# Conditioning clamps one unit earlier, a re-ordered opening with its products on GpSimd, activations laid out by batch, and the second batch's gates inside the unit loop

## The reference

```python
def bi_wkv(r, k, v, w, u, c):            # called twice: w = cond, then cond2; k = v = f
    tf = sigmoid(sum(c)); decay = exp(-exp(w)) * (0.5 + 0.5 * tf)
    ek = exp(min(k, 30)); ekv = ek * v
    nf, df = forward scans  of ekv, ek:  a = a * decay + x_t
    nb, db = backward scans of ekv, ek
    euk = exp(min(u + k, 30))
    return sigmoid(r) * (nf + nb - ekv + euk * v) / max(df + db - ek + euk, 1e-8) * (0.8 + 0.2 * tf)

y   = bi_wkv(x, f, f, ...)               # the cond stage
x  += W_O @ softmax(mask(K Q^T) / sqrt(128)) V        # 16 heads of 128, from y, causal
y2  = bi_wkv(x, f, f, ...)               # the cond2 stage
out = x + sum over the top 2 of 8 experts of gate * (y2 @ expert_w + expert_b)
```

## Time and profile before

| what | value |
|---|---|
| median of 3 runs | 398.97 us |
| the profiled execution | 399.12 us |
| its span | 397.3 us |
| TensorE busy | 366.3 us, 92% of the span |
| DVE / ACT / POOL busy | 306.8 / 224.5 / 187.5 us |
| mean granted TensorE clock | 0.991 of full speed |

### The profile page before, as it was taken

How to read it: one execution, slowest core, us unless ns; L and a number is a source line. 1 busy time by engine, 2 the same in 40 slices (tenths; PEclk the granted TensorE clock), 3 DMA queues, 4 the chain that set the end, 5 groups by cost and what they waited for, 6 DMA issues and landing times.

```text
span 397.3 us, 7668 instructions
## 1 busy us (share of the span) xinstructions
PE 366.3 (92%) x2600; PEld 340.9 (86%) x2600; DVE 306.8 (77%) x836; ACT 224.5 (57%) x613; POOL 187.5 (47%) x213
## 2 busy tenths in 40 slices
PE   0886989998999899979998999899999999999996
PEld 0775979998999899979997999899999989777885
DVE  4999978887787888778878887888757583677565
ACT  4647777557756757575767665866666463121000
POOL 1677866434634456656555655556664343010000
PEclk9996999999999999999999999999999999999999
DMA  7550220100000000120100004100000000000000
GB/s 246 192 196 18 74 85 4 53 2 1 2 2 0 2 2 0 54 81 27 55 0 2 0 9 155 53 2 2 1 2 0 2 0 2 2 0 26 28 26 27
DMA packets 5430, 14.27 MB, mean 36 GB/s; under 512 B 776, under 2 KB 2960, under 8 KB 4752
## 3 DMA queue, kind: packets, MB, share of 16 engines
q1 hardware_dynamic: 5248, 13.78, 10.3%
q10 hardware_dynamic: 144, 0.00, 0.0%
HBM read 12.73 MB, written 1.05 MB: 35 GB/s over the span
## 4 chain that ended last, share of the span: by engine, by line
PE 74%; DVE 17%; issue 4%; ACT 3%; DMA 1%; DVEq 0%; SPq 0%
PE psQK L840 8%; PE psQK L841 8%; PE psQK L842 8%; PE psS L840 5%; PE psS L842 5%; PE psS L841 5%; PE psT L900 4%; PE psO L841 4%; PE psO L842 4%; PE psO L840 4%; PE psV L840 3%; PE psZ L840 3%; PE psV L842 3%; PE psV L841 3%; PE psZ L841 3%
## 5 line engine op out<-in xcount | busy, mean ns | idle before, releaser
L452 ACT ACTIVATE prob<-prob,ntop 128x128 f32<-128x128 f32 (+1 forms) x128 | 57.3, 448 | 81.9 <-DVE ntop L679 81.9
L287 POOL TENSOR_SCALAR prob<-prob,rsum 128x128 f32<-128x128 f32 x64 | 38.6, 604 | 135.2 <-DVE rsum L686 135.2
L840 PE MATMUL psQK<-y_hi,w_hi 128*128 128x256 f32 x256 | 73.0, 285 | 2.2 <-DVE y_lo L599 2.2
L841 PE MATMUL psQK<-y_lo,w_hi 128*128 128x256 f32 x256 | 72.8, 284 | 0.0
L842 PE MATMUL psQK<-y_hi,w_lo 128*128 128x256 f32 x256 | 72.7, 284 | 0.0
L288 POOL TENSOR_SCALAR prob<-prob,rsum 128x256 f32<-128x256 f32 x64 | 59.1, 924 | 0.0
L261 POOL TENSOR_TENSOR w_lo<-raw,w_hi 128x512 fp32r<-128x512 f32 x40 | 51.9, 1309 | 12.7 <-ACT w_hi L339 12.6
L840 PEld LDWEIGHTS psQK<-y_hi,w_hi 128*128 128x128 f32 x256 | 49.5, 193 | 2.7 <-issue 2.5
L842 PEld LDWEIGHTS psQK<-y_hi,w_lo 128*128 128x128 f32 x256 | 49.5, 193 | 0.0
L841 PEld LDWEIGHTS psQK<-y_lo,w_hi 128*128 128x128 f32 x256 | 49.5, 193 | 0.0
L690 DVE TENSOR_TENSOR qk_lo<-psQK,qk_hi 128x512 fp32r<-128x512 f32 x64 | 43.6, 682 | 4.9 <-ACT qk_hi L440 4.2
(11 more groups left out here) (164 smaller groups left out, 1053.6 us busy)
## 6 DMA issues: line engine op xcount, KB each, us to landing
raw<-in_weights SPq DMA_DIRECT2D x5, 1024.0 KB, 6.5
raw<-in_weights SPq DMA_DIRECT2D x10, 512.0 KB, 4.4
out<-fT SPq DMA_DIRECT2D x8, 128.0 KB, 1.7
fT<-in_fT SPq DMA_DIRECT2D x2, 256.0 KB, 5.9
xT<-in_xT SPq DMA_DIRECT2D x2, 256.0 KB, 7.3
fT<-in_fT SPq DMA_DIRECT2D x1, 512.0 KB, 8.8
xT<-in_xT SPq DMA_DIRECT2D x1, 512.0 KB, 9.6
temb<-in_temb SPq DMA_DIRECT2D x1, 128.0 KB, 3.2
```

Source lines behind the costliest of these rows:

```text
L287: pool.tensor_scalar(prob[:, k, 0:P], prob[:, k, 0:P], rsum[:, k, 0:1], None, ALU.mult)
L452: ins = act.activation(prob[:, k, lo:hi], prob[:, k, lo:hi], ACT.Exp, scale=-1.0, bias=ntop[:, k, q:q + 1], accum_out=ssum[:, k, q:q + 1])
L840: pe.matmul(out, ah, bh, start=first and k == 0, stop=False)
L841: pe.matmul(out, ah, bl, start=False, stop=False)
```

## The change

1. The clamp of passes 2 to 7 moves on DVE from unit start - 1 to unit start - 2; ACT's exponentials stay.
2. Pass 1 is spread over units 0 to 4 in full: its two forward scan pairs move from ahead of unit 0 into it, its exponentials on ACT come after `qk_high(1)`, its clamp after `first_y_low(1)`. The first refills are in another order.
3. In the prologue the two products and the clamp of euk go to POOL, working on SBUF tiles, so ACT makes both exponentials twice (once to SBUF, once to PSUM); DVE does only the small steps that decay of stage 1 needs ahead of the first scans, and the rest behind them; the sums of c come from a matmul with ones and a small transfer; 14 dummy products instead of 16 start later and write another bank.
4. xT, fT, num2, y2, y_hi and y_lo are [P, B, CB, T] instead of [P, CB, B * T]; the host lays the inputs out to match.
5. `logits(1)` goes to unit 62 with a bank of its own (psQK[0]), batch 1's gates to units 62 and 63, `experts(0)` and `gates_turn(0)` to the end of unit 62, `base(0)` and `experts(1)` to that of unit 63, with `psE` in another order.

```diff
-DVE_PLACES = {"min": (-1, "E"), "xd": (0, "M"), ...
+DVE_PLACES = {"min": (-2, "E"), "xd": (0, "M"), ...
-DVE_FIRST = {"gd": (0, "M"), "gn": (0, "E"), "den": (1, "M"), "r0": (2, "M"), "r1": (3, "M"), "y": (4, "M")}
-ACT_FIRST = {"sxn": (0, "M"), "e1": (0, "E"), "yhi": (4, "E")}
-POOL_FIRST = {"eukv": 1, "y_low": 5}
+DVE_FIRST = {"xd": (0, "M"), "xn": (0, "E"), "gd": (1, "M"), "gn": (1, "E"), "den": (2, "M"), "r0": (2, "E"), "r1": (3, "M"), "y": (4, "M")}
+ACT_FIRST = {"sxd": (0, "E"), "sxn": (1, "M"), "e1": (1, "E"), "yhi": (4, "E")}
+POOL_FIRST = {"ekv": 0, "clamp": 1, "eukv": 4, "y_low": 5}
-REFILL = {1: (("qk", 0, 0), ("qk", 1, 0), ("qk", 2, 1), ("qk", 3, 2), ("v", 0, 1), ("v", 1, 2), ...
+REFILL = {1: (("qk", 0, 0), ("qk", 1, 1), ("v", 0, 1), ("qk", 2, 2), ("v", 1, 2), ("qk", 3, 3), ...
-WARM = 8
+WARM = 7
-    psE = [psQK[1], psQK[0], psS[0], psS[1]]
+    psE = [psQK[1], psS[0], psS[1], psQK[0]]
+    psL = [psV, psQK[0], psV, psV]
...
 # gpsimd, prologue, ahead of the refills
+        pool.wait_ge(f_act, 2)
+        pool.tensor_tensor(t0[:, EKV], t0[:, EK], cols(fT, 0), ALU.mult).then_inc(f_pool, 1)
+        pool.wait_ge(f_act, 4)
+        pool.tensor_scalar(t0[:, EUK], t0[:, EUK], EXP_LIMIT, None, ALU.min).then_inc(f_pool, 1)
+        pool.wait_ge(f_pool, 2)
+        pool.tensor_tensor(f_eukv, t0[:, EUK], cols(fT, 0), ALU.mult).then_inc(f_pool, 1)
...
 # scalar
-        at(62, "E", gates_copy, 0)
-        at(62, "E", base_copy, 0)
+        at(62, "E", gate_exp, 1)
+        at(63, "M", gates_copy, 0)
+        at(63, "E", gates_copy, 1)
+        at(63, "E", base_copy, 0)
...
 # vector
-        dve.tensor_tensor(f_ekv, f_ek, f0, ALU.mult).then_inc(f_dve, 1)
...
+        for c in range(CB):
+            dve.tensor_scalar(decay[:, 1, c], tdec[:], ew[:, 1, c:c + 1], None, ALU.mult).then_inc(pre_dve, 1)
...
+        dve.wait_ge(f_pool, 1)
+        for c in range(CB):
+            forward(f_xn[c], t0[:, EKV, c], 0, c, 0).then_inc(f_dve, 1)
...
-        dve.scalar_tensor_tensor(f_eukv, f_euk, EXP_LIMIT, f0, ALU.min, ALU.mult).then_inc(f_dve, 1)
...
-        second["min"]()
...
+        cond(1)["min"]()
         dve.wait_ge(consts, 3 + E)
-        second["xd"]()
         qk_low(0)
-        second["xn"]()
         qk_low(1)
...
+        at(62, "M", gate_first, 1)
+        at(62, "E", gate_last, 1)
+        at(63, "E", add_experts, 0)
...
 # tensor, unit loop and after it
+            if u == UNITS - 2:
+                logits(1)
...
-            if u == UNITS - 2:
-                gates_turn(0)
+            if u == UNITS - 1:
+                gates_turn(1)
...
             if u == UNITS - 2:
+                experts(0)
+                gates_turn(0)
+            if u == UNITS - 1:
                 base(0)
-                experts(0)
-        logits(1)
-        experts(1)
+                experts(1)
         experts(2)
```

More of the change, by code:

```diff
@@ L174, in cols @@
     def cols(t, b):
-        return t[:, :, b * T:(b + 1) * T]
+        return t[:, b]
     def halves(bank):
         return bank[:].rearrange("p (c n) -> p c n", c=2)
-    f_ek, f_ekv, f_euk, f_eukv = (halves(bank) for bank in (psQK[0], psQK[1], psS[0], psT))
+    f_ek, f_euk = halves(psQK[0]), halves(psS[0])
     f_xd, f_xn = [psV[:, 0:T], psS[1][:, 0:T]], [psZ[:, 0:T], psO[:, 0:T]]
-    f_e1 = tiles[:, 0, EK]
+    t0 = tiles[:, 0]
+    f_e1, f_eukv = t0[:, XD], t0[:, XN]
     def w_view(t, kind, part):
@@ L313, in _ @@
         at(62, y2_low, 1)
+        pool.wait_ge(f_act, 2)
[4 more added lines that the diff above has]
+        pool.tensor_tensor(f_eukv, t0[:, EUK], cols(fT, 0), ALU.mult).then_inc(f_pool, 1)
         for h in range(GH):
             refill("qk", 0, h)
[L317 to L323, removed]
+        for kind in ("v", "o"):
+            for part in range(2):
+                refill(kind, 0, part)
         for u in range(UNITS):
@@ L492, in do @@
                 f(*args)
[L494 to L499, removed]
+        for c in range(CB):
+            act.wait_ge(f_dve, 16 + 4 * c)
+            act.activation(y_hi[:, 0, c], f_xn[c], ACT.Copy).then_inc(f_act, 1)
         for part in range(2):
@@ L503, in _ @@
         qk_high(1)
-        second["sxd"]()
+        cond(1)["exps"]()
         for u in range(UNITS):
@@ L565, in backward @@
             return dve.tensor_tensor_scan(out[:, ::-1], dec(w, c, b), x[:, ::-1], 0.0, ALU.mult, ALU.add)
-        t0, f0 = tiles[:, 0], cols(fT, 0)
+        dve.wait_ge(pre_dve, 5)
         dve.wait_ge(f_act, 1)
@@ L880, in project_v @@
                 pe.wait_ge(gate_step, 1)
-            k = b * T + t * P
-            three(psV[:], [(both(y_hi, y_lo, ALL, c, slice(k, k + P)),
+            three(psV[:], [(both(y_hi, y_lo, ALL, b, c, slice(t * P, (t + 1) * P)),
                             both(w_hi, w_lo, ALL, g % 2, SLOT_V, c)) for c in range(CB)]).then_inc(v_done, 1)
@@ L925, in logits @@
         def logits(b):
+            bank = psL[b]
             if b == 0:
@@ L934, in logits @@
             for t in range(TT):
-                n, o = b * T + t * P, (b * TT + t) * E
+                o = (b * TT + t) * E
                 for c in range(CB):
-                    ins = pe.matmul(psG[:, o:o + E], y2[:, c, n:n + P], gate_w[:, c], start=c == 0, stop=c == CB - 1)
+                    ins = pe.matmul(bank[:, o:o + E], y2[:, b, c, t * P:(t + 1) * P], gate_w[:, c], start=c == 0, stop=c == CB - 1)
             ins.then_inc(logits_done, 1)
@@ L962, in base @@
             for t in range(TT):
-                n = b * T + t * P
                 for c in range(CB):
-                    pe.matmul(out[:, t * C + c * P:t * C + (c + 1) * P], xT[:, c, n:n + P], identf[:],
+                    pe.matmul(out[:, t * C + c * P:t * C + (c + 1) * P], xT[:, b, c, t * P:(t + 1) * P], identf[:],
                               start=t == 0 and c == 0, stop=False, is_transpose=True)
@@ L1031, in _ @@
         experts(4)
-        gates_turn(1)
         experts(5)
@@ L1069, in lay_out @@
         "fT": channels_first(inputs["fside_BxSxS_0"]),
-        "temb": np.ascontiguousarray(inputs["cond_512"]),
+        "temb": np.ascontiguousarray(inputs["cond_512"].T),
         "wu": np.ascontiguousarray(wu),
```

157 lines of the change are left out of this document (79 added, 78 removed).

## The result

| kernel | median | runs | profiled execution, span |
|---|---|---|---|
| before | 398.98 us | 4 runs, 398.76 to 399.33 | 399.12, 397.3 |
| after | 391.85 us | 4 runs, 391.55 to 392.67 | 392.67, 389.9 |

The ratio is 0.982 (95% interval 0.981 to 0.984): 7.1 us faster, where 11.8 were forecast. The time lies inside the range given, near its slow end. In the spans of the profiled executions the gain is 7.4. The four spans of the changed kernel are 389.6 to 389.9, and 1.9 to 2.8 us of its executions lie around them, against 1.8 before.

The account below looks back on a forecast made before the run. TensorE was taken as the bound, waiting at pass starts, with DVE setting the pace until about 50 us. Terms 9.5 + 2.0 + 0 + 0.3 = 11.8 take 399.1 to 387.3 us; own range 384.5 to 389.5, wider range 383.5 to 392.

Parts of the forecast that it names:

- Step 1: Passes 2 to 7: clamps two units ahead remove TensorE's paired idles at pass starts; gain 9.5 us, ends 4.0 and 12.0.
- second idle: TensorE's later wait at each pass start, for V's second half: 4.2 of 6.5 us goes, about 2.3 stays.
- laps: Overlap between matmuls lost at each TensorE wait: 0.25 us per first wait and 0.2 per second.
- Step 2: Prologue: TensorE's restart on channels 1 moves from 22.50 to 20.7 us, a gain of 1.8, ends -0.5 and 3.8.
- its own signs: Prologue: right if DVE's first instruction comes between 4.3 and 5.3 us; wrong if scans of ekv last over 1 us.
- f lands earlier by 1.1: Opening loads: 1 KB instead of 128 KB ahead and 2 KB pieces bring f 0 to 1.8 us earlier; 1.1 taken.
- two such meetings cost 1.3: Prologue: `first_y` adds two SBUF tiles beside POOL's weight subtractions; two stalls cost 0 to 2.5 us, 1.3 taken.
- 2.0 for DVE's shorter chain: Prologue: two products (0.6 each) and the clamp (0.8) leave DVE's chain, 2.0 us.
- rival C: Prologue: by the SBUF page's rule POOL's clamp and product hold DVE's scans, together 2.4 us; 389.7 us, chance 0.04.
- B: Pass starts: the second idle stays, hanging on ACT's order within its unit, not the clamp; 391.5 us, chance 0.09.
- Step 3: Units 0 to 4: spreading pass 1 removes two idles, adds others before `values(0)` and `values(2)`; +0.2 us, ends -3.0 and 6.3.
- Step 5: Kernel end: `logits(1)` fills a 0.81 us idle, new `gates_turn(1)` wait about 1.0; net 0.3, ends -1.5 and 1.5.

Follow-up runs that it names:

- old_prologue: The changed kernel with the earlier kernel's DVE, ACT and POOL prologue, but pass 1 still spread over units 0 to 4; 389.53 us.
- old_opening: The changed kernel with the prologue and the placing of pass 1 of the kernel before; 389.36 us.
- both_ports: The changed kernel with the prologue's backward sums GN in PSUM and GpSimd's clamp and second product held until the scans of ekv are done; 389.52 us.
- host_as_before: The changed kernel with the opening of the kernel before, x and f in DRAM in the earlier order, in SBUF by batch; 387.60 us.
- ports_and_host: The whole change with GN in PSUM, GpSimd's clamp and second product after the scans of ekv, and x and f in DRAM as before; 388.23 us.
- all_but_clamps: The changed kernel with the clamps of passes 2 to 7 back at unit start - 1; 403.63 us, ratio 1.011 to the kernel before.

## Why the prediction was off

**Step 1 (9.5) held.** The clamps alone gave 10.0, at the five later passes 1.35 to 2.72 each. Two errors in it nearly cancel: my 4.2 for the second idle was too low, since only pass 2 kept one (1.1 us), and the laps too high. Of 9.3 us of booked idles 8.2 went, so the laps gave 1.8 where I had put 2.7.

**Step 2 (+1.8 at the restart) is the step that failed.** It came out as -2.1, by two of its terms, and of its own signs f's landing (6.26, where 4.3 to 5.3 was given) and the scans of ekv (1.01 and 1.69, where over 1 was to mean that the step is wrong) say so. "f lands earlier by 1.1" joined a part that was right (the small transfer, 1.0) to one with the wrong sign: the pieces of 2 KB, which I counted as help, cost 1.5 by their place in DRAM. And "two such meetings cost 1.3" should have been 3.5 in all: the two meetings booked, the adds of `first_y`, cost 0.7 and 1.1, and two places that were not in the sum cost the rest, the second scan of ekv 1.0 and the small steps 0.7. In the sum I had set the scans against GpSimd's clamp alone, though the same trace has two scans at 3.11 beside subtractions; that its second product follows right behind stood in rival C only, at a chance of 0.04. The 2.0 for DVE's shorter chain is right: 16.27 becomes 14.37 where only the meeting of the decay steps is left.

Rival C was the mechanism for a part of this. B's time, 391.5, is the nearest to what was measured, but its reason is wrong: the second idles went. C's rule (the Trainium skill, SBUF — State Buffer, Who interferes with whom) also bears on the small steps: it counts `tensor_scalar` among the operations that can enter a mode which takes the shared ports, where its operands allow it. The trace agrees in part: L573 and L578 took 0.54 and 0.56 beside GpSimd's clamp, 0.18 and 0.17 without, but L573 ended 0.86 before the clamp did, so it was not blocked to the end, and L575 (two SBUF inputs) and L576 were not longer at all. It agrees for the second scan and `first_y`; for two scans beside a clamp in the kernel before it does not the earlier trace rows.

**Step 3 (+0.2) had the right idles** (2.44 of the 3 before `values(0)`, 1.78 of the 2 later) and nearly the right sum, 0 by old_prologue against old_opening. But `values(0)` came 1.5 earlier and not 4 to 6, and its reason contradicts step 2: if DVE and what hangs on it set the pace up to unit 5, an earlier restart is worth nothing by itself. I booked 1.8 for it all the same. By both_ports, the prologue's 2.0 on DVE would not have reached the end even without these meetings, since the way through GpSimd and the weights is then the longer one; f's landing and the stalls did reach it.

**Step 5 (0.3)** came out as 0.6, the new wait of `gates_turn(1)` at 0.82 of the 1.0 forecast.

In the terms of the sum: clamps 10.0 for 9.5; opening about -3.3 (f -0.5, meetings -2.6 to -2.8 at maxima(5)) for +2.0; end 0.6 for 0.3. These make 7.3 of the 7.4 between the spans. That the time still lies in the range given, by 0.15 us, is owed to its slow end, which was set for the rivals; the forecast's own range, 384.5 to 389.5, missed it.

## What to carry to other kernels

A wait that recurs once per pass is best removed at its source, one small edit, before anything larger is built on top: here it was worth more than the whole change. Work moved to another engine to relieve a busy one should be laid against that engine's whole list at that time, row by row, since a meeting of the two can take back more than the work was, and against what waits in that engine's own queue, here the weights; and an earlier start is booked only if the stretch behind it is bound by the same thing. A layout is also an address pattern in DRAM: change it on chip and keep the host's order, or time the first landing.

## What was not expected of the hardware

- 256 KB read as 2 KB at every 8 KB of DRAM landed some 1.4 us later (6.17 to 6.31 us in seven kernels) than as 1 KB at every 4 KB (4.73 to 4.91 in four); pieces of 1 KB cut out of the former addresses were as late (6.24). All engines' transfers together moved 183 instead of 261 GB/s at 3 to 4 us. Why these addresses are slower stays open.
- A DVE `tensor_scalar` of 4 to 16 columns took 0.54 and 0.56 us beside a clamp on GpSimd, 0.17 to 0.18 without; two others beside the same clamp took 0.17 and 0.16 as usual.
- In the kernel before, a pair of scans took 1.27 us beside GpSimd's clamp in each of six passes, and 3.11 beside its subtractions of weights.
- A low stretch of the clock can cost nearly nothing: from f to maxima(5) host_as_before took 46.57 us with the granted clock at 1.00, ports_and_host 46.71 at 0.93. The two differ in more than the clock, so this is an argument and not a test; TensorE idles for others in that stretch. In all_but_clamps a low stretch went with 1.4 us.
